# Dense tap by spans of six rows, float32 scores in row groups, maxima from bf16 parts, one addition per gather: attention and deformable convolution on one core

## What is computed

```python
xn = group_norm(x, norm_w, norm_b)
q, k, v = split(einsum('bchw,oc->bohw', xn, qkv_w) + qkv_b)
attn = softmax(q @ k.T * hd ** -0.5)           # per head, 4096 x 4096
feat_l = einsum(attn @ v, proj_w) + proj_b + x
om = conv2d(conv2d(concat(feat_l, 2 * feat_s), W_off), W_om, pad=1) + b_om
o1, o2, mask = split(om, 3); mask = sigmoid(mask)
# per group (8), tap (9) and pixel: bilinear sample of feat_s at pixel + tap + offset, times mask
val = (four corners of feat_s weighted by (ly, lx)) * mask
out = relu(einsum('bgckhw,ogck->bohw', val, W_dcn) + b_dcn) + feat_l
```

## Time and profile before

| | us |
|---|---|
| median of 3 runs (12790.51 to 12822.48) | 12791.58 |
| the profiled execution | 12790.43 |
| its span, first to last instruction | 12788.6 |
| busy: PE, DVE, ACT, POOL | 8894.0, 7910.4, 2914.1, 10703.5 |
| a step in the middle, query product to query product | 378 |

### The profile page before, as it was taken

How to read it: one execution, slowest core, us unless ns; L and a number is a source line. 1 busy time by engine, 2 the same in 40 slices (tenths; PEclk the granted TensorE clock), 3 DMA queues, 4 the chain that set the end, 5 groups by cost and what they waited for, 6 DMA issues and landing times. The chain is left out here.

```text
span 12788.6 us, 126443 instructions
## 1 busy us (share of the span) xinstructions
PE 8894.0 (70%) x34036; PEld 3273.8 (26%) x34036; DVE 7910.4 (62%) x9169; ACT 2914.1 (23%) x3357; POOL 10703.5 (84%) x24581
## 2 busy tenths in 40 slices
PE   5666778765777767777666777766687766778732
PEld 1222222222222222222222222222232222222211
DVE  3466666666666666656666656666566666656633
ACT  2222222211222211222122222211222221222200
POOL 0488888887888888888788888888788888888888
PEclk8888888887888887888788888878788887888865
DMA  3222211112111111111211111111211111111111
GB/s 94 75 65 67 78 29 25 28 29 61 29 32 28 28 28 29 29 29 31 54 35 29 29 27 27 28 28 29 62 24 34 29 28 29 29 29 25 28 24 23
DMA packets 458806, 469.41 MB, mean 37 GB/s; under 512 B 150432, under 2 KB 274464, under 8 KB 458016
## 3 DMA queue, kind: packets, MB, share of 16 engines
q0 software_dynamic: 262144, 268.96, 10.3%
q1 hardware_dynamic: 97952, 119.95, 3.5%
q10 hardware_dynamic: 97920, 71.35, 1.8%
HBM read 390.46 MB, written 69.21 MB: 36 GB/s over the span
## 5 line engine op out<-in xcount | busy, mean ns | idle before, releaser
L408 POOL DMA_INDIRECT g<-patches,idx x8192 | 7862.1, 960 | 1254.6 <-issue 1180.1
L404 POOL TENSOR_TENSOR carrier<-carrier 128x1 f32<-128x1 f32 x15872 | 2766.3, 203 | 140.1
L982 DVE TENSOR_TENSOR ring<-ring,hats 128x1024 f32<-128x1024 f32 x1024 | 1259.3, 1230 | 2520.4 <-PE ring L655 2187.3
L494 ACT ACTIVATE p<-ring 128x1024 f32<-128x1024 f32 x2048 | 2089.2, 1022 | 2812.3 <-PE ring L622 1936.6
L597 PE MATMUL ring<-k,q 128*128 128x512 bf16 x4096 | 1763.9, 529 | 1216.2 <-DVE mx L844 796.3
L844 DVE TENSOR_REDUCE mx<-ring 128x1 f32<-128x1024 f32 x2048 | 2381.1, 1218 | 300.9 <-PE ring L597 300.9
L621 PE MATMUL ring<-q,k 128*128 128x512 bf16 x4096 | 1598.3, 390 | 307.3 <-ACT p L494 84.0
L622 PE MATMUL ring<-q,k 67*128 67x512 bf16 x4096 | 1584.9, 387 | 0.0
L655 PE MATMUL ring<-fx,hats 64*128 64x512 f32 x4096 | 1203.2, 666 | 230.8 <-ACT hats L482 178.8
L984 DVE TENSOR_REDUCE dval<-ring 128x16 f32<-128x1024 f32 x1024 | 1254.1, 1225 | 35.4
L678 PE MATMUL ps_a<-p,v 128*64 128x512 f32 x4096 | 1110.9, 621 | 2.0 <-ACT p L494 2.0
(11 more groups left out here) (117 smaller groups left out, 5707.2 us busy)
## 6 DMA issues: line engine op xcount, KB each, us to landing
g<-patches,idx POOLq DMA_INDIRECT x8192
patch_in<-in_fpad ACTq DMA_DIRECT2D x544, 64.0 KB
patches<-patch_out ACTq DMA_DIRECT2D x136, 256.0 KB
k<-k_parts SPq DMA_DIRECT2D x96, 256.0 KB
q<-q_parts SPq DMA_DIRECT2D x192, 128.0 KB
k_parts<-v SPq DMA_DIRECT2D x16, 768.0 KB
q_parts<-p SPq DMA_DIRECT2D x32, 384.0 KB, 2.6
p<-in_x SPq DMA_DIRECT2D x4, 2048.0 KB
```

Of the source, the lines that this page charges most:

```text
L404: last = nc.gpsimd.tensor_tensor(carrier[:, col:col + 1], carrier[:, 0:1], carrier[:, 0:1], ALU.add)
L408: nc.gpsimd.indirect_dma_start(out=g[:, part, j - CUTS[part] * GROUPS, :], out_offset=None, in_=patches[b], in_offset=bass.IndirectOffsetO ...
L494: nc.scalar.activation(p[:, n % 4, :, :], ring[u % 2][:, :, :], ACT.Exp, scale=SCALE)\
L982: then(V.tensor_tensor(cells, cells, hy[:, at * HEIGHT:(at + 1) * HEIGHT].unsqueeze(2).to_broadcast([128, HEIGHT, GC]), ALU.mult))
```

## The change

- **POOL:** `RESTS` goes from 2 to 1. There is one addition ahead of each gather. The four parts of g are one array with the same 4 x 16 gathers.
- **Sampling on VectorE:** w4 is written to `weights` in SBUF, so L962 reads g and weights, both in SBUF. `align` runs once per tile, with all nine taps, and the Relu writes `relu_out` in SBUF.
- **Scores:** q and k are kept once, in float32 (`kf`, `qf`), head h on partitions 32h to 32h+31, and no part goes through DRAM. In the loop four float32 products of 32 rows, one per head, go into four banks, and a bf16 product adds the maximum (`ones_b`, `mq`). A block takes both ring slots at once.
- **Maxima:** three bf16 products (high x high, high x low, low x high) of 32 rows accumulate per head; a chunk is 2 heads x 512 keys, still 128x1024 and 64 chunks.
- **Dense tap:** the y position is split into a span of rows (first row a multiple of 5) and a rest. For four groups at a time (a set), one plane of x hats and three planes of y hats of two rows each are made; VectorE multiplies them (`weigh_hats`, 128x1536, both inputs in SBUF), TensorE multiplies each hat with the feature rows of 13 spans (6 products of 128x208 for two groups, a half), into a bank of its own (`half_set`), and VectorE picks the right span (128x416) and sums. A set is made every four blocks.
- `points` has five more small operations on 128x8. `project` runs the `fs_s` product first.

```diff
-RUN, RESTS = 1, 2
+RUN, RESTS = 1, 1
...
-                w4 = turned[:, 512 - 4 * (j1 - j0):512]
+                w4 = weights[:, 0:4 * (j1 - j0)]
...
                 for c in range(USE_K):
-                    nc.scalar.activation(k_made[:, 0, :], ring[u % 2][:, :, :].rearrange("p i n -> p (i n)"), ACT.Identity,
-                                         bias=k_bias).then_inc(k_high, 1)
+                    for made in (kf, k_high):
+                        last = nc.scalar.activation(made[:, c * 1024:(c + 1) * 1024], ring[u % 2][:, :, :].rearrange("p i n -> p (i n)"),
+                                                    ACT.Identity, bias=k_bias)
...
+            def make_hats(s, b, t, i):
+                k = hat_use(s, t, i)
+                wait_slot_full(act, before_att(s, b, k), k)
+                made = hats[:, i % 2, :, :]
+                nc.scalar.activation(made[:, 0, :], ring[k % 2][:, 0, :], ACT.Abs, bias=plus_x, scale=-1.0)
+                for pair in range(PAIRS):
+                    last = nc.scalar.activation(made[:, 1 + pair, :], ring[k % 2][:, 1, :], ACT.Abs, bias=pair_rows[:, pair:pair + 1],
+                                                scale=-1.0)
+                last.then_inc(ring_free[k % 2], 1)
+                wait_slot_read(act, before_att(s, b, k), k)
+                for half in range(2):
+                    part = made[:, 2 * half:2 * half + 2, :].rearrange("p v n -> p (v n)")
+                    last = nc.scalar.activation(part, part, ACT.Relu, bias=ones_s[:, 0:1], scale=-1.0)
...
+                            for n, (q_part, k_part) in enumerate(((q_high, k_high), (q_high, k_low), (q_low, k_high))):
+                                for i in range(2):
+                                    rows = slice((2 * pair + i) * HD, (2 * pair + i + 1) * HD)
+                                    last = mm(ring[u % 2][:, i, :], q_part[rows, sub * 128:(sub + 1) * 128],
+                                              k_part[rows, c * 512:(c + 1) * 512], start=n == 0, stop=n == 2)
...
+            def scores(s, b, kt):
+                n = slice(kt * 128, (kt + 1) * 128)
+                uses = [score_use(s, kt, pair) for pair in range(2)]
+                for pair in range(2):
+                    u = uses[pair]
+                    wait_slot_free(pe, before_att(s, b, u), u)
+                    for i in range(2):
+                        rows = slice((2 * pair + i) * HD, (2 * pair + i + 1) * HD)
+                        mm(ring[u % 2][:, i, :], kf[rows, n], qf[rows, :], start=True, stop=False)
+                for pair in range(2):
+                    u = uses[pair]
+                    for i in range(2):
+                        rows = slice((2 * pair + i) * HD, (2 * pair + i + 1) * HD)
+                        last = mm(ring[u % 2][:, i, :], ones_b[rows, :], mq[rows, :], start=False, stop=True)
+                    last.then_inc(ring_full, 1)
...
+            def weigh_hats(s, b, t, i):
+                dve.wait_ge(hats_ready, tile_number(s - 1, t) * SETS + i + 1)
+                made = hats[:, i % 2, :, :]
+                V.tensor_tensor(made[:, 1:, :], made[:, 1:, :], made[:, 0:1, :].to_broadcast([128, PAIRS, SET_GROUPS * 128]), ALU.mult)\
+                    .then_inc(hats_weighed, 1)
```

More of the change, by code:

```diff
@@ L48 @@
 USES_ATT = USES_PLAIN + SUB * USE_D
-HALF = HEIGHT // 2
+SETS = 2 * DENSE
+SET_GROUPS = GROUPS // 2
+SET_AT = tuple(i * KT_TILE // SETS for i in range(SETS))
+BLOCK = 5
+BLOCKS = -(-HEIGHT // BLOCK)
+PAIRS = (BLOCK + 1) // 2
+UNITS = DENSE * GROUPS
 PICKS = PICKED * GROUPS
@@ L659, in scores, with distances @@
-            def scores(s, b, kt, fresh):
-                t, j = divmod(kt, KT_TILE)
-                dense = t in dense_tiles(s)
-                if dense and j == 0:
-                    distances(s, b, t)
-                for pair in range(2):
-                    scores_of_pair(s, b, kt, pair)
-                    if dense and pair < DENSE:
-                        columns_of_group(s, b, t, j, pair, fresh)
+            def distances(s, b, t, i):
+                if i == 0:
+                    pe.wait_ge(idx_ready[t], uses_of(s - 1, t))
+                k = hat_use(s, t, i)
+                wait_slot_free(pe, before_att(s, b, k), k)
+                for axis in range(2):
+                    for j in range(SET_GROUPS):
+                        at = i * SET_GROUPS + j
+                        last = mm(ring[k % 2][:, axis, j * 128:(j + 1) * 128],
+                                  dpos[:, t, 1 - axis, at:at + 1].to_broadcast([128, 128]), ident_s[:, :], start=True, stop=True)
+                last.then_inc(ring_full, 1)
@@ new lines, in blocks_of_half @@
+            def blocks_of_half(s, b, t, i, half, fresh):
+                number = half_number(s, t, i, half)
+                if positive(number):
+                    pe.wait_ge(half_used, number)
+                if half == 0:
+                    pe.wait_ge(hats_weighed, tile_number(s - 1, t) * SETS + i + 1)
+                    if fresh and t == 1 and i == 0:
+                        pe.wait_ge(fx_loaded, (b + 1) * (16 * (BLOCK + 1)))
+                for u in range(2):
+                    j = 2 * half + u
+                    group = (i % 2) * SET_GROUPS + j
+                    cells = half_set[:, u * 256:u * 256 + BLOCKS * GC].rearrange("p (y c) -> p y c", c=GC)
+                    for pair in range(PAIRS):
+                        last = mm(cells, hats[:, i % 2, 1 + pair, j * 128:(j + 1) * 128], fx[:, pair, :, group * GC:(group + 1) * GC],
+                                  start=pair == 0, stop=pair == PAIRS - 1)
+                last.then_inc(half_full, 1)
@@ L669, in weigh, with dense_work @@
+            def dense_work(s, b, kt, fresh):
+                for t, i in hats_at(s, kt):
+                    distances(s, b, t, i)
+                for t, i, half in sets_at(s, kt):
+                    blocks_of_half(s, b, t, i, half, fresh)
             def weigh(s, b, kt):
@@ L769, in _ @@
             walk(pe, prepare, step, 2)
-            align(STEPS * SUB - 1, PARTS - 1)
+            align(STEPS * SUB - 1)
         @block.vector
```

379 lines of the change are left out of this document (158 added, 221 removed).

## The result

The changed kernel takes 12,246.8 us (median of 4 runs, 12,245.5 to 12,256.4) against 12,794.4 beside it: a ratio of 0.957, 95% interval 0.9553 to 0.9586. The profiled execution took 12,247.7, its span is 12,245.9.

A forecast was written before the change was run, and what follows sets the result against it. POOL's chain of gathers was taken as the bound. From 12,790: -40 (first gather) - 1180 (additions) - 98 (waits) + 737 (two-SBUF-input contention) = -581, so 12,209 us; range 11,450 to 12,680, some 8 in 10.

The forecast's parts named there:

- Additions: POOL's gather loop (L404): one addition less per gather, period 1.470 to 1.326 us, 1180 us saved.
- Rival 1: The addition was free: gathers behind one addition start no sooner; 13,390 us, slower; chance 0.10.
- the step that bounded this term: Additions' saving put between 0 and 1180 us; 1180 taken, since gather 0.95 and gap 0.15 are the same in every period.
- POOL is the bound, the rest needs 363: Kernel before, per step: POOL needs 376 us, the rest of the kernel alone some 363, only 4% lower.
- The second SBUF input: VectorE products L962 and L975, both inputs in SBUF, hold POOL up: 717 us, plus 20 for small ones.
- The count behind it: L788's twelve full-length runs beside gathers in the old trace: 0.25 to 0.98 us lost each, 0.63 on average.
- Rival 2: The second input costs nothing in the loop, L962 falling beside gathers, not additions; 11,470 us; chance 0.09.
- the prediction's reading: A gather of 1.76 us beside L788 says descriptor generation is not spared by a product with two SBUF inputs.
- POOL's waits for val: POOL's nine waits for buffers that VectorE gives back: 279.5 us shrink to 180, put as -98.
- First gather: Start of POOL's first gather: 40 us earlier, near 352 us, mostly because the k parts' trip goes.
- The chain behind POOL: Rest of the kernel without POOL: from 363 to 330 us per step, 32 below POOL's 362.
- Rivals 3 and 4: TensorE's row groups take turns: 13,970 us, chance 0.05; chain behind POOL 45 us per step longer: 12,625 us, chance 0.12.

The follow-up runs named there:

- 14,884: Kernel before, with its second addition before every second gather only: 14,883.8 us, ratio 1.160.

## Why the prediction was right, point by point

The predicted 12,209 us is 38 below the measured time, within its range. The terms of the sum held in size. What it took for granted, that a faster stream of gathers leaves the other engines alone, did not hold in any other kernel tried, and that it held in this one is luck.

- **Additions.** Predicted a period of 1.326, measured 1.333: -1,122 instead of -1,180. Rival 1 is out, since gathers behind one addition do start sooner. But the step that bounded this term was incomplete. I argued that gather and gap stay as they are, so the gain lies between 0 and 1,180, and never asked what else a faster stream of gathers does. In the kernel before that one line costs 3,580 us (16,375 against 12,795). The reading "POOL is the bound, the rest needs 363" is shown at the old rate alone.
- **The second SBUF input.** Predicted 737, measured 607 (667 less the 60 that were there). L975 loses 1.34 us against my 1.3. L962 loses 0.53 against my 0.75, and 0.82 in the kernel before with two additions: my 0.75 came from rows with pairs of additions and is near for them. The count behind it was low: with every lengthened record beside them, gathers included, the twelve runs of L788 lose 0.58 to 1.24 us, 0.92 on average, where I had 0.63. Rival 2 is out. The gather of 2.47 us beside L975 bears out what the one of 1.76 us had shown. The Trainium skill (SBUF — State Buffer, Who interferes with whom) infers that descriptor generation is spared by such a product. These rows show that the gather instruction is not; but it also reads its indices (`idx`) from SBUF, and whether it waits in that read or in making its descriptors they do not tell, so the prediction's reading went too far.
- **The two terms as independent ones.** Taking either part of the contention away costs 3,870 or 4,470 us, where the sum gives a gain of some 200 or 340. It would be tempting to say that the contention keeps the changed kernel on time. The traces don't show that: both variants are late from 376 us on, before the first product with two SBUF inputs in the loop. The contention's price is measured where nothing else is wrong: +362 us in the kernel before, and 208 saved with two additions.
- **POOL's waits for val.** Predicted 180, measured 296 in 36 waits. The longest, in the first step, is 106.6 against 86.6 before: POOL reaches the same wait sooner. Too low by 116, and with the additions' +58 this offsets the contention's -130.
- **First gather.** 352 predicted, 356.2 measured.
- **The chain behind POOL.** 330 predicted, some 343 measured. Measured over the steps (medians, gather waits included) the stages changed by -9 (queries, -9 predicted), +17 (maxima, 0 to +10 predicted), -8 (from there to the loop, -7), -20 (loop, -18) and +4 (end, +1). The maxima are outside my bounds: the 64 reductions start 1.39 us apart (mean of the periods under 2 us) instead of 1.16, which is 15 of the 17; my upper end stood for 1.32, and with the clock at 0.50 TensorE needs more. None of it reaches the end time. Rivals 3 and 4 are out: L655 runs its four row groups side by side, and POOL's step is 362, the number predicted.
- **The range.** No rival in it stood for what the experiments found, a kernel a third slower. It held because the changed kernel happens to be on time, for a reason that is not known.

## What to carry to other kernels

Where an engine issues indirect gathers back to back, idle work between them may be what keeps TensorE's results on time. Thin it out a little at a time, and watch the waits of the engines that read TensorE's products as well as the gathers' period: if they grow while TensorE's records have long ended, the gathers are too close. Before explaining why a variant is slow, look for the first microsecond at which its trace differs. Here that was before the edit had acted, and it ruled out the explanation that the table suggests. And run the kernel that is the exception again beside its variants.

## What the runs showed of the hardware

- With fewer additions between gathers of 128 rows, TensorE's finished products reach VectorE and ScalarE late in nine of the ten kernels tried, by 20 us and more in most of them, once by 34 us with nothing else running. The lateness grows while gathers go by, and after they stop it ends within some 5 us. VectorE's and ScalarE's signals are not delayed by more than 0.16 us in the median. The bf16 maxima are late as well, 21.8 us with gathers 1.333 us apart.
- TensorE itself can be slowed: weight loads 1.4 us apart where 0.22 was the rule just before, half of the offsets' product in 47.7 us instead of 9.8 at most.
- What holds the signal back is open. The gathers' own transfers are no later: from the end of a gather's record to its last packet the median is 1.15 us in the changed kernel and 1.15 in those of 14,884 and 16,375 us. Whether it takes many small products or a full ring behind them was not told apart, nor whether the recording of the profile takes part. Nor is it known why the changed kernel is on time.
- A product of two SBUF inputs holds up a gather as well as an addition (2.47 us instead of 0.96), and its cost depends on what stands between the gathers: 0.53 us with one addition, 0.70 with two in the same kernel.
- Six bf16 products of 32 rows per chunk, in pairs, kept TensorE 94% busy at a granted clock of 0.50 where two of 128 rows left it 60% busy at 0.91.
- No version tried beats the changed kernel. Three of its variants are late from the first maxima on, where their gathers are the same as its own, so its time may not be a safe one.
